# Slot-order stores with paired gathers in attention, W1 products in place of constants, and W2's load held for W1

## The reference

```python
x = x + 0.5 * ffn(layernorm(x))     # f1
x = x + attention(layernorm(x))     # at
x = x + 0.5 * ffn(layernorm(x))     # f2

# ffn: 2048 tokens, 8 experts, the two best of each token
p = softmax(xt @ Wr + br); probs, idx = top_k(p, 2); probs /= probs.sum(-1)
h = layernorm(relu(xt @ W1[e] + b1[e])) * g1[e] + be1[e]      # 128 -> 512
y = layernorm(relu(h @ W2[e] + b2[e])) * g2[e] + be2[e]       # 512 -> 128
out = sum of probs * y over the two experts of the token

# attention: 8 heads, two causal softmaxes per head
w = softmax(q1 @ k1.T) - lam * softmax(q2 @ k2.T)
o = w @ v; o = o * rsqrt(mean(o*o) + eps) * (1 - lambda_init); return o @ Wo.T
```

## Time and profile before

| what | value |
|---|---|
| median of 3 runs | 533.02 us (532.73 to 536.91) |
| the profiled execution | 534.94 us, its span 533.2 us |
| f1: head, pairs | 0 to 51 us, 51 to 175 us |
| attention | 175 to 342 us |
| f2: head, pairs, end | 342 to 383 us, 383 to 503 us, 503 to 533 us |
| PE busy | 456.2 us (86%) |
| DVE, ACT, POOL busy | 357.5, 291.5 and 226.3 us |
| DMA | 24.19 MB, mean 45 GB/s |

### The profile page before, as it was taken

How to read it: one execution, slowest core, us unless ns; L and a number is a source line. 1 busy time by engine, 2 the same in 40 slices (tenths; PEclk the granted TensorE clock), 3 DMA queues, 4 the chain that set the end, 5 groups by cost and what they waited for, 6 DMA issues and landing times.

```text
span 533.2 us, 11962 instructions
## 1 busy us (share of the span) xinstructions
PE 456.2 (86%) x3800; PEld 307.8 (58%) x3801; DVE 357.5 (67%) x1259; ACT 291.5 (55%) x587; POOL 226.3 (42%) x282
## 2 busy tenths in 40 slices
PE   8999988877888987888898898679997887787995
PEld 7653666656666444555555565464555665565654
DVE  5795666666667567787887775667826666666864
ACT  2484955555455256778777774551054555555640
POOL 8664566566633222044224102120155655565430
PEclk9989988998889999999999996998799889999998
DMA  8901111111110310000000000001011111112016
GB/s 251 292 2 33 38 43 41 39 39 42 39 27 31 116 38 5 19 1 3 2 0 0 1 1 1 1 2 80 5 46 42 39 39 39 39 44 39 26 47 218
DMA packets 13734, 24.19 MB, mean 45 GB/s; under 512 B 3466, under 2 KB 6210, under 8 KB 13443
## 3 DMA queue, kind: packets, MB, share of 16 engines
q1 hardware_dynamic: 8306, 12.93, 7.7%
q0 software_dynamic: 5392, 10.80, 7.2%
HBM read 15.43 MB, written 8.26 MB: 44 GB/s over the span
## 4 chain that ended last, share of the span: by engine, by line
PE 39%; DVE 22%; ACT 14%; issue 10%; another core or an unknown queue 8%; DMA 3%; DVEq 2%; POOL 2%; ACTq 0%; SPq 0%; POOLq 0%
PE bank L606 5%; DVE mx L1340 4%; ACT wide L435 4%; DVE st L800 4%; PE bank L588 3%; PE bank L519 2%; PE bank L597 2%; ACT wide L992 2%; ACT early L1000 2%; PE bank L1608 2%; PE bank L1181 2%; PE bank L1142 2%; DVE yy L817 2%; ACT hT L457 2%
## 5 line engine op out<-in xcount | busy, mean ns | idle before, releaser
L606 PE MATMUL bank<-w2c,hT 128*128 x624 | 86.9, 298 | 36.0 <-ACT hT L457 33.7
L606 PEld LDWEIGHTS bank<-w2c,hT 128*128 128x128 f32 x624 | 81.9, 210 | 61.5 <-issue 61.5
L318 POOL DMA_INDIRECT xg<-xn_scratch,slot_u x78 | 75.5, 968 | 89.5 <-DVE slot_u L764 37.9
L325 POOL DMA_INDIRECT y_scratch<-yo,dest_u x78 | 77.1, 989 | 66.2 <-ACT yo L450 49.6
L457 ACT COPY hT<-bank 128x1024 f32<-128x1024 f32 (+1 forms) x40 | 39.6, 989 | 79.3 <-remote 53.9
L588 PE MATMUL bank<-w1s,xT 128*128 x156 | 74.0, 596 | 0.6 <-DVE w2c L1493 0.6
L1340 DVE TENSOR_REDUCE mx<-bank 128x4 f32<-128x1024 f32 (+1 forms) x48 | 58.4, 1221 | 19.1 <-PE bank L1151 19.1
L1000 ACT ACTIVATE early<-bank 128x768 f32<-128x768 f32 x64 | 51.8, 812 | 24.7 <-PE bank L1171 24.3
L800 DVE BATCH_NORM_STATS2 st<-wide 128x6 f32<-128x512 f32 x78 | 50.2, 685 | 19.7 <-ACT wide L435 12.6
L817 DVE SCALAR_TENSOR_TENSOR yy<-bank,r,b2p 128x128 f32<-128x128 f32 x78 | 24.6, 351 | 48.3 <-remote 42.1
L597 PE MATMUL bank<-ident,wide 128*128 128x128 f32 x312 | 45.4, 292 | 3.3 <-ACT wide L435 2.6
(11 more groups left out here) (286 smaller groups left out, 868.9 us busy)
## 6 DMA issues: line engine op xcount, KB each, us to landing
w1s<-in_L_ffn_W_dram SPq DMA_DIRECT2D x1, 2048.0 KB, 9.4
xn_scratch<-xn SPq DMA_DIRECT2D x2, 1024.0 KB, 4.7
yk<-y_scratch SPq DMA_DIRECT2D x8, 256.0 KB, 2.8
early<-y_scratch SPq DMA_DIRECT2D x8, 256.0 KB, 3.6
xg<-xn_scratch,slot_u POOLq DMA_INDIRECT x78
y_scratch<-yo,dest_u POOLq DMA_INDIRECT x78
out_dram<-xs SPq DMA_DIRECT2D x8, 128.0 KB, 2.7
g2b<-in_L_ffn_g_dram POOLq DMA_DIRECT2D x1, 512.0 KB, 5.5
```

The costliest lines, as they stand in the source:

```text
L318: pool.indirect_dma_start(out=xg[:, u, :], out_offset=None, in_=xn_dram, in_offset=bass.IndirectOffsetOnAxis(ap=slot_u[:, n:n + 1], axis=0 ...
L325: pool.indirect_dma_start(out=y_dram, out_offset=bass.IndirectOffsetOnAxis(ap=dest_u[:, 2 * p + j:2 * p + j + 1], axis=0), in_=yo[:, p % 2 ...
L606: last = pe.matmul(bank[7][:, j * DIM:(j + 1) * DIM], hT[:, u, j, c * P:(c + 1) * P], w2c[:, bass.ds(e * (FC * DIM) + c * DIM, DIM)], star ...
```

## The change

It has four parts.

1. In f1 POOL no longer scatters. SP stores each finished pair into y_scratch as it is, in the order of the slots, with one plain transfer of 128 KB (64 KB for the last). POOL only gathers in f1, and `dest_u` isn't made there.
2. In attention the two rows of each token are now fetched by POOL with indirect gathers by `posi`, four per batch (128 rows, 64 KB each), 32 in all, in place of SP's 8 plain loads. Four stand ahead of turn 0, the others among POOL's work, in pairs, up to turn 5. `early_combine(1)` moves on DVE from behind `norm(0)` to behind `pieces(0)`, and the `keep_warm` ahead of the first layer norm grows from 47 to 59 matmuls.
3. In f1's head, the two `keep_warm(3, 5)` between the logits give way to W1's centring products of experts 0 and 1; those of expert 2 and 3 and the bias products follow, so that one expert's product more stands ahead of the counts. SP waits until W1 has landed before it issues W2's load and all that stands behind it.
4. In both MoE stages the one-hots are built in 2 groups of 16 columns.

The core of the diff:

```diff
-        def moe_sync(sp, S, first, last):
+        def moe_sync(sp, S, first):
 ...
+            if first:
+                for p in range(PAIRS):
+                    k = min(2, SLOT_TILES - 2 * p)
+                    sp.wait_ge(S["yf"], p + 1)
+                    sp.dma_start(y_dram[2 * p * P:(2 * p + k) * P, :].rearrange("(j p) d -> p j d", p=P), yo[:, p % 2, 0:k, :]
+                                 ).then_inc(S[f"yst{p % 2}"], 16)
+                return
@@ moe_gpsimd
+            if first:
+                for p in range(PAIRS - 4):
+                    pool.wait_ge(S["xTp"], p + 3)
+                    for j in tiles[p + 4]:
+                        gather(2 * p + 8 + j, 2 * (p % 2) + j)
+                return
             pool.wait_ge(S["dest"], 1)
@@ finish, on ACT
-                    act.wait_ge(S[f"yst{u}"], (m - u) * 16)
+                    act.wait_ge(S[f"yst{u}"], (m - u) * (8 if first else 16))
@@ PE, the head
                     logits(pe, S, g - 1, first)
                     if g < 3:
-                        keep_warm(3, 5)
+                        center_product(pe, g - 1)
 ...
             if first:
-                hidden_weights(pe, range(0, 3))
+                center_product(pe, 2)
+                for e in range(3):
+                    bias_product(pe, e)
+                hidden_weights(pe, range(3, 4))
 ...
-                hidden_weights(pe, range(3, 6))
+                hidden_weights(pe, range(4, 6))
 ...
             for c in range(TOPK * TT):
-                if c % 8 == 0:
-                    pe.wait_ge(S["oh"], c // 8 + 1)
+                if c % 16 == 0:
+                    pe.wait_ge(S["oh"], c // 16 + 1)
@@ DVE, the one-hots
-            for q in range(4):
-                c = slice(8 * q, 8 * q + 8)
+            for q in range(2):
+                c = slice(16 * q, 16 * q + 16)
@@ att_gpsimd
+            def rows(b, ks):
+                if ks[0] == 0 and b >= 3:
+                    pool.wait_ge(S[f"yld{b % 2}"], landed(b) - ROWS)
+                if ks[0] == 0 and b >= YRING:
+                    pool.wait_ge(S["comb"], b - YRING + 1)
+                if ks[0] == 1:
+                    pool.wait_ge(S[f"yld{b % 2}"], landed(b) - ROWS // 2)
+                for k in ks:
+                    for t in (2 * b, 2 * b + 1):
+                        c = k * TT + t
+                        pool.indirect_dma_start(out=yk4[:, t % (2 * YRING), k, :], out_offset=None, in_=y_dram[0:SLOT_TILES * P, :],
+                                                in_offset=bass.IndirectOffsetOnAxis(ap=posi[:, c:c + 1], axis=0)
+                                                ).then_inc(first_row(t, k)[0] if b == 0 else S[f"yld{b % 2}"], 16)
 ...
+            pool.wait_ge(S["yst0"], 8 * PAIRS)
+            pool.wait_ge(S["yst1"], 8 * PAIRS)
+            rows(0, (0, 1))
             for t in range(BATCH + 3):
                 if A_:
                     pool.wait_ge(A["var"], t + 1)
                     pool.tensor_tensor(ars[:], ave[:], neg_half[:, 0:2], ALU.pow).then_inc(A["rs"], 1)
+                if t == 0:
+                    rows(1, (0,))
+                    rows(1, (1,))
+                    pool.wait_ge(S["yld1"], landed(1))
+                    rows(2, (0,))
+                if t == 1:
+                    rows(2, (1,))
+                if 2 <= t < BATCH - 2:
+                    rows(t + 2, (0,))
                 if A_ and t not in (0, BATCH - 1):
                     pool.wait_ge(A["xn"], t + 1)
                     combine(t + 1)
                 if D_ and t != BATCH + 2:
                     pool.wait_ge(A["msq"], t - 2)
                     pool.tensor_tensor(orr[:], oms[:], neg_half[:, 0:2 * HEADS], ALU.pow).then_inc(A["rms"], 1)
+                if t == 1:
+                    rows(3, (0,))
+                if 1 <= t < BATCH - 2:
+                    rows(t + 2, (1,))
@@ PE, attention
-            keep_warm(47)
+            keep_warm(59)
@@ SP, the loads
             sp.dma_start(w1s[:] ...).then_inc(s_ld_w1, 16)
+            sp.wait_ge(s_ld_w1, 16)
             sp.dma_start(w2s[:] ...).then_inc(s_ld_w2, 16)
```

More of the change, by code:

```diff
@@ L278, in build, with landed, first_row, loads @@
         NMASK = 18
-        LOADED = [(0, 0), (4 * 16, 4 * 16, 0, 0)]
-        def loads(b, last):
-            ring = [sems[k][n] for k in (("f1", "f2") if last else ("f1",)) for n in ("yld0", "yld1")]
-            return ring[b % len(ring)], LOADED[last][b % len(ring)] + 16 * (b // len(ring) + 1)
-        def moe_sync(sp, S, first, last):
+        ROWS = 16 * 2 * TOPK
+        def landed(b):
+            return (b // 2 + b % 2) * ROWS
+        def first_row(t, k):
+            u = TOPK * t + k
+            return sems["f1"][f"xg{u}"], 16 * len(range(u, SLOT_TILES, 4)) + 16
+        def loads(b):
+            ring = (sems["f2"]["yld0"], sems["f2"]["yld1"], sems["f1"]["dest"], s_ld_w2)
+            return ring[b % 4], 16 * (b // 4 + 1) + (16 if b % 4 == 3 else 0)
+        def moe_sync(sp, S, first):
             sp.wait_ge(S["xn"], TT)
             sp.dma_start(xn_dram.rearrange("(p t) d -> p t d", p=P), xn[:]).then_inc(S["xnst"], 16)
+            if first:
[5 more added lines that the diff above has]
+                return
             sp.wait_ge(S["yst0"], 16 * PAIRS)
@@ L774, in moe_vector @@
             ins.then_inc(S["eid"], 1)
-            step(dve.scalar_tensor_tensor(dest_f[:], slot_f[:], 0.0, spare[:], ALU.is_equal, ALU.mult))
-            dve.tensor_tensor(dest_u[:], dest_f[:], slot_f[:], ALU.add).then_inc(S["dest"], 1)
+            if not first:
+                step(dve.scalar_tensor_tensor(dest_f[:], slot_f[:], 0.0, spare[:], ALU.is_equal, ALU.mult))
+                dve.tensor_tensor(dest_u[:], dest_f[:], slot_f[:], ALU.add).then_inc(S["dest"], 1)
             dve.wait_ge(S["gexp"], 1)
@@ L1276, in early_combine @@
                 S = sems["f1"]
-                dve.wait_ge(*loads(b, False))
+                if b:
+                    dve.wait_ge(S["yld1"], landed(1))
                 for k in range(TOPK):
                     for t in range(2 * b, 2 * b + 2):
+                        if b == 0:
+                            dve.wait_ge(*first_row(t, k))
                         if k:
@@ L1413, in turn @@
                     norm(t)
-                if isinstance(t, int) and t == 0:
-                    early_combine(1)
                 if B_:
@@ L1438, in turn @@
                     pieces(t)
+                if isinstance(t, int) and t == 0:
+                    early_combine(1)
                 if D_:
```

55 lines of the change are left out of this document (26 added, 29 removed).

## The result

The changed kernel took 525.13 us in the median of 4 runs (523.57 to 526.19), the kernel before 532.88 beside it: a ratio of 0.9863, with a 95% interval of 0.982 to 0.9905. The prediction was 513.

The account below looks back on a forecast made before the run. The prediction took PE's signals, held back by POOL's bursts of indirect transfers, as the bound. It summed -22.4 (f1's pairs), +2.4 (boundary) and -0.2 (heads) to -20.2 us, giving 513 us, range 507 to 530 at 0.80.

Parts of the forecast that it names:

- The bound: f1 and f2 pair loops: PE's finished turn_h signal is held back until POOL's burst of six indirect transfers drains; 53.9 us.
- Part 1: f1's pair loop: without scatters the pauses go, 14 pairs cost 4.92 us in place of 6.52, -22.4 us.
- The boundary: Between f1 and attention: last store, four gathers and the longer keep_warm delay PE's first turn, +2.4 us.
- Attention behind it: Attention's turns: gathers fit POOL's idle time, 0, bound 1 us; early_combine(1) off the critical path, 0, bound +1.
- The head: Heads of both MoE stages: centring products for warmers and two one-hot groups, -0.2 us, bounds -1 and +1.
- The loop rival: f1's pair loop: the hardware loop makes the pauses, so f1 keeps its 22.4 us; 535.2 us, chance 0.18.
- POOL becomes the bound of attention: Attention: slower gathers or landing waits ahead of orr cost four or five turns 2 us each; 522 us, chance 0.07.
- The pauses shrink only: f1: signals late behind two gathers too, or another wait takes over; half of 22.4 kept, 524 us, chance 0.07.

Follow-up runs that it names:

- dummy_gathers_f1: f1_plain plus two unread gathers per pair in f1, where the two scatters had stood: 535.36 us, ratio 1.0051 to the kernel before.
- scatters_only: Kernel before with f1's gathers replaced by SP's plain loads of other rows, the 39 scatters kept: 510.97 us, ratio 0.9542.
- f1_plain_2: f1_plain run again, on a chip where the kernel before takes 534.22 us: 511.81 us, ratio 0.9558.
- after_again: The changed kernel, unchanged, run again on a chip where the kernel before takes 533.33 us: 521.73 us, ratio 0.9797.
- after_no_hold: The changed kernel with W2's load issued at once, not after W1's landing; centring products stay between the logits: 521.05 us in a single run.
- after_third: The changed kernel, unchanged, on a chip where the kernel before takes 489.61 us: 497.28 us, ratio 1.0177.
- f1_plain_dummy_att_2: f1_plain plus 32 unread gathers in attention at the change's places, where the kernel before shows f1's pauses: 521.09 us, ratio 0.9704.
- after_fourth: The changed kernel, unchanged, on another chip, where the kernel before takes 489.36 us: 494.29 us, ratio 1.0091.
- f1_plain: Kernel before with SP's plain slot-order stores for f1's scatters, attention's plain loads kept, sorting back omitted: 488.97 us against 490.38, ratio 1.001.

## Why the prediction was wrong

**The bound: right, on its kind of chip.** The wait for remote was PE's signal held back by a burst of POOL's indirect transfers. dummy_gathers_f1 and scatters_only show it from both sides. That other chips run the same kernel without it could not be seen in one trace, and the prediction had no rival for it.

**Part 1, -22.4: right.** Measured alone 22.4 us (f1_plain_2), within the changed kernel 21.0 by the landmarks. The cost of a pair, 4.92, was right (4.93).

**The boundary, +2.4: right**, +1.9 in this profile, by the working given: store, four gathers, and a keep_warm that ends just as DVE is ready.

**Attention behind it, 0 with a bound of 2 us: this is the step that failed.** It cost 9.4 us in the predicted run, and 8.5 and 7.8 in the profiles of after_again and after_no_hold, on a holding chip too (from the ars of turn 0 to that of turn 7, against the first profile). By its own signs the prediction was wrong here: attention grew by more than 4 us, and POOL had no idle time ahead of ars in turns 1 and 2. The sum priced 28 gathers by POOL's time only, 2.6 us against 2.48 of slack, and took the rest for hidden. Four things were left out. The first is the largest; how the 9.4 us divide among them is not measured one by one.

First, its own finding. If a burst holds PE's signals in f1, gathers can hold them in attention too. The timeline of a steady turn after the change:

```profile
223.46 0.97 POOL L971 DMA_INDIRECT yk<-y_scratch,posi  x1 [0.30 <-issue]
223.50 0.22 PE L1200 MATMUL bank<-wide 48*128 48x128 bf16 x2
223.61 0.22 PE L1200 MATMUL bank<-wide 48*128 48x128 bf16 x2
224.43 0.65 ACT L1107 CAST hT<-hT 128x512 bf16<-128x512 f32 x1
225.03 1.23 DVE L1392 TENSOR_REDUCE mx<-bank 128x4 f32<-128x1024 f32 x1 [0.87 <-PE bank L1200]
```

The last product ends at 223.83, and DVE, idle for the last 0.87 us, starts on it at 225.03, 1.2 us later; a gather had just been issued. At the same place on a free chip (after_third) the gap is 0.05 us:

```profile
218.06 0.97 POOL L971 DMA_INDIRECT yk<-y_scratch,posi  x1 [0.30 <-issue]
...
218.90 0.22 PE L1200 MATMUL bank<-wide 48*128 48x128 bf16 x2
...
219.01 0.22 PE L1200 MATMUL bank<-wide 48*128 48x128 bf16 x2
...
219.28 1.23 DVE L1392 TENSOR_REDUCE mx<-bank 128x4 f32<-128x1024 f32 x1 [0.36 <-PE bank L1200]
```

This is no single case. Between the ars of turn 0 and that of turn 7 of the predicted run there are 14 places where DVE or ACT starts 0.6 to 1.4 us behind the signal of PE that ended its wait, with a gather just issued or under way; 11 of them lie ahead of 250 us, where the stage takes its first loop branch. after_again has 13 of them and f1_plain_dummy_att_2 has 12. The kernel before, f1_plain_2 and every kernel on a free chip have none over 0.3 us. Without late signals, on free chips, the changed kernel needs 118.1 us for these turns (after_third, after_fourth), against 123.6 to 125.3 on holding ones: 5.5 to 7.2 us for this and for the clock, which was granted at 0.89 and 0.92 in two of the turns. The dummies' difference between the kinds, 9.6 against 4.5 us, says about the same. Not every signal beside a gather is late, though, and here pairs of gathers are enough, where in scatters_only pairs of scatters were not; what decides it is open.

Second, early_combine(1), which the sum put at nothing. Before, DVE did it in a wait for ACT at 184.35. Now its rows are gathered from 167.23 on, and it stands, 1.14 us long and with no idle time around it, straight in front of turn 1's statistics, on which ars waits. The prediction had it done about a microsecond before they are needed. The turn from the first ars to the second grew from 9.63 to 11.23 us, and to 11.30 on a free chip (after_third).

Third, the waits for landed rows. Six gathers in turn 0 were priced at 7.8 us against 8.89 of idle time. With their two waits of 1.75 and 1.84 us they fill 10.3, and ars stands behind them (timeline of DVE and POOL, predicted run):

```profile
171.26 0.95 POOL L971 DMA_INDIRECT yk<-y_scratch,posi  x1 [1.75 <-DMA yk<-y_scratch,posi]
...
175.08 1.14 DVE L1334 SCALAR_TENSOR_TENSOR xs<-yk,gate,xs 128x128 f32<-128x128 f32 x4
175.31 0.95 POOL L971 DMA_INDIRECT yk<-y_scratch,posi  x1 [1.84 <-DMA yk<-y_scratch,posi]
176.25 0.49 DVE L1343 BATCH_NORM_STATS2 ast<-xs 128x6 f32<-128x128 f32 x2
...
177.06 0.17 DVE L1351 TENSOR_SCALAR ave<-amv 128x2 f32<-128x2 f32 x1
...
177.54 0.73 POOL L1000 TENSOR_TENSOR ars<-ave,neg_half 128x2 f32<-128x2 f32 x1
```

But DVE was late itself: ave ends at 177.23, so ars starts 0.31 us behind it in turn 1, and 0.42 in turn 2, against 0.08 before: no more than 0.6 us of ars's delay in this run is the queue's. It is 1.8 to 2.0 us in four other profiles of the same attention code (after_again, after_no_hold, after_third, after_fourth), nearly all of it in turn 2.

Fourth, what the late rows move. combine(2) now waits for them until 183.29, and so runs beside DVE's large operations:

```profile
183.37 1.39 DVE L1366 TENSOR_SCALAR hT<-hT 128x512 f32<-128x512 f32 x1
...
183.44 1.04 POOL L979 TENSOR_TENSOR yk<-yk,gate 128x512 f32<-128x512 f32 x1
...
185.71 0.71 POOL L985 TENSOR_TENSOR xs<-xs,ysum 128x256 f32<-128x256 f32 x1
185.82 1.16 DVE L1370 TENSOR_TENSOR hT<-hT 128x512 f32<-128x512 f32 x1
```

In turn 1 of the kernel before the same two took 0.43 and 0.68 us, with combine long done, so this is 1.4 us more on DVE (the whole turn grew by 1.0, 14.78 to 15.80). The Trainium skill, page "SBUF — State Buffer", section "Who interferes with whom", says that a DVE tensor_scalar in a 2-port mode, or a DVE operation with two SBUF inputs, and a GpSimd operation that reads SBUF exclude each other for the whole instruction. The trace agrees: DVE's two operations are longer by 0.96 and 0.48 us, and within them POOL's operations run for 1.04 and 0.60 us.

**The head, -0.2: wrong in this run**, +2.4. The text had the landing of W1 at 15.58 and the first product at 15.24, and took that for a wait of 0.35 us. W1 landed at 16.4, 0.9 us later than in the profile of before, and the place has no slack: PE's order then delays the logits, and in this run the clock fell behind it. Over all profiles the new head is about 1.1 us later than the old one.

**f2 and the last turns**, +1.9 and -3.4, go with the clock, which the sum didn't have and which differs between executions: f2's pairs are 1.7 us longer at 0.94 granted against 0.96, the last turns 3.4 shorter at 0.97 against 0.89. Without the -3.4 the result would have been further from 513.

**The rivals.** The loop rival, 0.18, is dead: the loop stands in every kernel here, and f1's pauses left with the bursts. The 535 us that the prediction drew from the Trainium skill's page "Runtime: NRT & Kernel Launch" did not come either: f1_plain_2 and the changed kernel run through the same loop without a pause. "POOL becomes the bound of attention", 522 at 0.07, came nearest in size and place, but not by its mechanism: orr starts 0.08 us behind DVE's oms in every turn, as before, and what the queue delays is ars. "The pauses shrink only" had the right idea, a signal late behind a pair of gathers, and looked for it in f1 alone, where it didn't happen.

## What to carry to other kernels

When a trace shows that one kind of work disturbs another, price every place to which the change moves that work by the disturbance too, not by its own duration. A wait inside a queue counts with the queue: transfers with waits for landed rows between them cost their landing times, not their issue times. Work that moves from a wait to a place without one costs its whole length, as early_combine(1) did. And a large wait whose releaser the profile can't name may not be there on another chip: look at the same kernel on one before a change is built on it, for here the same edit is 1.4 to 2.0% faster on one kind and 0.9 to 1.8% slower on the other.

## What the hardware showed

- The kernel before runs in 533 or in 490 us, three series of each. The difference of 43 to 44 us is about what the pauses of f1 and f2 cost: 22.4 us in f1 (f1_plain_2), and f1_plain, without those, still takes 22.8 us less on a free chip than on a holding one (488.97 against 511.81).
- On holding chips signals of PE wait while POOL's indirect transfers follow each other: ACT idles 3.9 us behind a burst of six, and in attention DVE and ACT start 0.6 to 1.4 us late beside pairs of gathers, at 12 to 14 places. With pairs of scatters (scatters_only) nothing is late.
- On free chips an unbroken run of such transfers for the whole of f2's loop delays nothing.
- W1's 2 MB landed 9.4 to 11.3 us after their issue (after_again and after_no_hold).
- Why a chip holds, and what holds, is open: no run here changes anything on the chip's side.
